# A graph network's opening phase: the encoder also skips block 11, and the early sums are dealt out anew

## What is computed

```python
h = jnp.maximum(_layernorm(x), 0.0)
h = jnp.maximum(h @ enc_w1.T + enc_b1, 0.0) @ enc_w2.T + enc_b2       # the encoder
def step(h, w):                                                       # five of these
    m = h @ w
    agg = jax.ops.segment_sum(m[src], dst, num_segments=n_nodes)      # a sum over edges
    gi = agg @ gru_wih.T + gru_bih
    gh = h @ gru_whh.T + gru_bhh
    ...
h, _ = jax.lax.scan(step, h, conv_w)
...
x = x + jax.nn.sigmoid(out)
...                                    # then the second network, with two more edge sums
```

## Time and profile before

| | us |
|---|---|
| median of three runs (745.25 to 745.31) | 745.26 |
| the profiled execution's own time | 745.62 |
| its span, first to last instruction | 743.3 |
| PE busy | 721.4 |
| DVE busy | 335.2 |
| ACT busy | 315.2 |
| clock granted to TensorE, mean | 0.999 of full |

### The profile page before, as it was taken

How to read it: one execution, slowest core, us unless ns; L and a number is a source line. 1 busy time by engine, 2 the same in 40 slices (tenths; PEclk the granted TensorE clock), 3 DMA queues, 4 the chain that set the end, 5 groups by cost and what they waited for, 6 DMA issues and landing times.

```text
span 743.3 us, 9918 instructions
## 1 busy us (share of the span) xinstructions
PE 721.4 (97%) x4071; PEld 394.4 (53%) x4071; DVE 335.2 (45%) x677; ACT 315.2 (42%) x463; POOL 44.5 (6%) x56
## 2 busy tenths in 40 slices
PE   6889999999999999999999999999999999999997
PEld 3556666445444444444444444444445545558886
DVE  7999999525023241123231223646644631123432
ACT  3977877645344344234452334432447421212000
POOL 4240000000000000000000000120002210000000
PEclk9999999999999999999999999999999999999999
DMA  5020000734102332022230212710002000000100
GB/s 164 6 84 16 4 2 5 147 69 81 9 1 55 63 51 46 1 48 39 53 75 0 49 37 38 115 63 2 1 0 97 9 1 1 1 1 6 34 31 25
DMA packets 79240, 28.41 MB, mean 38 GB/s; under 512 B 70519, under 2 KB 78390, under 8 KB 79062
## 3 DMA queue, kind: packets, MB, share of 16 engines
q1 hardware_dynamic: 78230, 26.93, 17.2%
q0 software_dynamic: 240, 0.66, 0.3%
q10 hardware_dynamic: 720, 0.13, 0.1%
HBM read 8.03 MB, written 2.60 MB: 14 GB/s over the span
## 4 chain that ended last, share of the span: by engine, by line
PE 85%; DVE 9%; ACT 2%; DMA 2%; POOL 1%; issue 1%; SPq 0%; DVEq 0%; ACTq 0%; POOLq 0%
PE PSA L1241 35%; PE PSA L1458 9%; PE PSA L1323 7%; PE PSA L1402 5%; PE PSA L1186 4%; PE PSA L1254 3%; PE PSA L1263 3%; PE PSA L1258 3%; PE PSA L1262 3%; PE PSA L1256 3%; PE PSA L1265 3%; DVE CT L869 3%; PE PSA L1390 2%; PE PSA L1378 1%; DMA H<-yS 1%; DVE stat L834 1%
## 5 line engine op out<-in xcount | busy, mean ns | idle before, releaser
L1241 PE MATMUL PSA<-AT,H 128*128 128x512 fp8e3 (+1 forms) x1470 | 275.8, 347 | 0.8 <-DMA H<-yS 0.8
L1241 PEld LDWEIGHTS PSA<-AT,H 128*128 128x128 f16 x1470 | 126.8, 98 | 151.9 <-issue 12.0
L1078 DVE SCALAR_TENSOR_TENSOR rS<-PSA,bias,rS 128x512 f32<-128x512 f32 (+1 forms) x35 | 23.9, 682 | 261.6 <-ACT rS L1635 261.6
L1635 ACT ACTIVATE rS<-PSA,bias 128x512 f32<-128x512 f32 (+1 forms) x35 | 22.1, 632 | 199.6 <-PE PSA L1262 199.6
L869 DVE TENSOR_TENSOR CT<-CT 128x2048 bf16<-128x2048 bf16 x80 | 91.4, 1206 | 0.0
L1565 ACT ACTIVATE AT<-PSA 128x1000 fp8e3<-128x1000 f32 (+1 forms) x79 | 74.4, 997 | 20.7 <-PE PSA L1186 20.5
L1539 ACT ACTIVATE CTL<-AT 128x3125 fp8e3<-128x3125 fp8e3 (+1 forms) x25 | 69.9, 2797 | 0.0
L1402 PE MATMUL PSA<-CT,H 128*128 128x512 fp8e3 (+1 forms) x336 | 65.5, 351 | 0.3 <-POOL H L762 0.3
L1458 PE MATMUL PSA<-AT,CT 128*128 128x256 f16 x576 | 65.1, 273 | 0.6 <-DVE AT L1040 0.6
L1458 PEld LDWEIGHTS PSA<-AT,CT 128*128 128x128 fp8e3 x576 | 55.4, 98 | 7.2 <-DVE AT L1040 0.8
L1323 PE MATMUL PSA<-AT,H 128*128 128x512 fp8e3 x245 | 58.0, 379 | 1.2 <-ACT AT L1565 1.2
(11 more groups left out here) (181 smaller groups left out, 661.8 us busy)
## 6 DMA issues: line engine op xcount, KB each, us to landing
AT<-scale_scratch SPq DMA_DIRECT2D x1, 1562.5 KB, 6.5
H<-in_x SPq DMA_DIRECT2D x1, 1536.0 KB
out<-AT SPq DMA_DIRECT2D x12, 128.0 KB
comb_scratch<-CT SPq DMA_DIRECT2D x1, 960.0 KB, 4.5
comb<-comb_scratch SPq DMA_DIRECT2D x5, 192.0 KB, 2.5
H<-yS SPq DMA_TRANSPOSE x48, 2.5
H<-in_x SPq DMA_DIRECT2D x1, 512.0 KB, 4.9
CT<-AT SPq DMA_TRANSPOSE x25, 4.0
```

What stands on the lines that cost most here:

```text
L1241: last = nc.tensor.matmul(bank[:, 0:w], H16[:, l % 2, t, h, :], AT3[:, t, n0:n0 + w], start=(t == 0 and h == 0), stop=(t == T - 1))
```

## The change

`REST` becomes a pair, so the encoder has no step in block 11 either, and every step from 11 on moves one block later. All that is tied to `block_of` moves along: `first_norm(6)` from block 10 to 11, `normalized(6)` from 11 to 12, and `low_encoded` of chunks 3 to 6 by one block each. `PART` deals the early sums out anew up to block 22: chunk 0's sum ends in block 20 instead of 18, and chunk 1's begins in block 16 instead of 13; from block 23 on nothing changes. ACT's copy of the first sum (`aggregated(0)`, L1627) follows from block 19 to block 21. The wait of `transposed_keys(2)` is set to the number of states that are written by then.

```diff
-        REST = 7
-        step = lambda b: b - ENC - (b > REST) if b != REST else None
+        REST = (7, 11)
+        step = lambda b: b - ENC - sum(b > r for r in REST) if b not in REST else None
...
-        PART = {7: [(0, 0, 4)], 8: [(0, 4, 8)], 10: [(0, 8, 12)], 12: [(0, 12, 16)], 13: [(1, 0, 4)], 14: [(0, 16, 20)],
-                15: [(1, 4, 8)], 16: [(0, 20, 24)], 17: [(1, 8, 11)], 18: [(0, 24, T), (1, 11, 13)]}
-        PART.update({19 + i: [(1, 13 + 3 * i, 16 + 3 * i)] for i in range(4)})
+        PART = {7: [(0, 0, 4)], 8: [(0, 4, 8)], 10: [(0, 8, 10)], 11: [(0, 10, 12)], 13: [(0, 12, 14)], 14: [(0, 14, 16)],
+                15: [(0, 16, 20)], 16: [(1, 0, 4)], 17: [(1, 4, 8)], 18: [(0, 20, 24)], 19: [(1, 8, 12)],
+                20: [(0, 24, T), (1, 12, 15)], 21: [(1, 15, 20)], 22: [(1, 20, T)]}
...
-                    pe.wait_ge(state_encoded, (3, 6, NC, NC)[k - 1])
+                    pe.wait_ge(state_encoded, (3, 5, NC, NC)[k - 1])
```

## The result

The changed kernel takes **750.53 us** (median of six runs, 747.92 to 751.13) against 745.23 for the kernel before in the same runs: a ratio of 1.0067, 95% interval 1.0056 to 1.0077, or **+5.3 us**. Forecast were +2.9 us and 747.0 to 749.3. The sign was right, the size was not, and the time lies above the range. The profiled execution took 750.48, its span is 748.3.

What follows compares the result with a forecast made beforehand. PE was taken as the bound from 64.5 us on, DVE just before. Lost early matmuls 2.59 plus a missing encoder step 0.62, less 0.27 already gained, gave +2.9 on 745.26: 748.2 us, range 747.0 to 749.3.

Steps and rivals of the forecast that it cites:

- The method: Opening blocks: sum PE's idle time from block 10 until it never waits again, 4.5 us against 1.45 before.
- DVE's dates: Blocks 12 and 13: DVE never idles, finishing block 12's one-hots at 56.55 and block 13's at 61.16 us.
- the key wait at L1215: Block 13: PE idles 1.6 us until ACT has copied the keys transposed just before.
- nothing behind block 22 absorbed or added anything: After block 14 PE runs without a gap, so the 2.9 us shift carries through to the end.
- So I add nothing: Stalls of 1.8 and 1.6 us on PE leave its clock at 2.4 GHz, so no time is added.
- the row from 5.7 to 11 us: Profile window of the kernel before: PE busy 2.05 of 5.30 us, clock granted at 1.00, cited against a clock fall.
- the prediction's dates: PE's expected times: block 13's one-hots at 61.29, L1215 going on at 64.25, block 14's head at 66.07 us.
- rival D: Clock falls in blocks 12 to 14, adding 3 to 5 us: 751 to 753 us, chance 0.07.
- stalls of 0.45, 1.8 and 1.6 us: PE idles 0.45 at L1228 in block 12, 1.8 ahead of block 13, 1.6 at L1215 in block 13.
- B: Chunk 1's old 1.34 us stall in block 13 goes and nothing replaces it: 743.9 us, chance 0.04.
- C: Later PE slack of some 3 us makes the moved matmuls free, leaving 0.3 us: 745.6 us, chance 0.07.
- handoffs: Five passes of work between engines, each good to 0.1 to 0.2 us, taken as unknowns beside the key wait.

Runs made afterwards that it cites:

- e1: The changed kernel plus seven unused 512-column matmuls in block 12, where PE idled ahead of block 13: 747.66 us, ratio 1.0034.
- e2: The kernel before, its encoder resting in block 7 only, with the new table of early sums: 746.07 us, ratio 1.0013.
- e3: The changed kernel's encoder pauses in blocks 7 and 11, with early sums as near to the old table as the waits allow: 746.68 us, ratio 1.0022.
- e4: The changed kernel with the third group's keys made in block 13 instead of 12, and the matching wait count: 746.05 us, ratio 1.0012.
- The halves: Two runs, each with one part of the change: the new table alone (e2), 746.07 us, and the encoder's second pause alone (e3), 746.68 us.
- r_after: The changed kernel measured again, unaltered, beside other runs on one chip: 750.56 us, ratio 1.0073.
- e8: The changed kernel with three tiles of chunk 0's early sum moved from blocks 13 to 15 into block 12, no work added: 747.07 us.
- e6: e1 with POOL's eight small memsets moved ahead of its last root: 747.63 us.

## Why the prediction was wrong

**The method held.** Idle time of PE up to the point from which it is saturated was the right sum, and it gave what it was to give wherever the clock stayed up: in e1, which is the changed kernel with its clock, the first L1254 came 3.03 us later than in before, for a forecast of 2.9 (by the time 747.66, for 748.2); e2, e3 and e4 came within 0.4 us, all on the low side. DVE's dates were right to 0.1 us but for POOL's memsets, which the prediction passed over: it moved POOL's last root, and not the memsets behind it, which then fell on the keys. Of the waits, the key wait at L1215 was foreseen with 1.6 and measured with 1.46 (e1), and in the changed kernel nothing behind block 22 absorbed or added anything: the first L1254 is 5.02 us later in the changed kernel (134.61 against 129.59), and the span 5.0 longer. The halves show that both parts of the change cost, and why: the table takes eight matmuls out of block 12, where DVE sets the date, and the pause brings the key copy and its reader into one block.

**The step that failed is the one on the clock.** "So I add nothing" stood on the row from 5.7 to 11 us, in which PE is busy 2.05 of 5.30 us and the column reads 1.00. That row did not show what it was read for, because PE was not at full speed there. The costs of the matmuls say so. These are rows of before:

```profile
7.39 1.58 PE L1163 MATMUL PSA<-CT 125*128 125x86 f32 x6 [1.22 <-DVE CT L807]
...
15.04 1.86 PE L1186 MATMUL PSA<-CT 128*128 128x125 bf16 x16
16.70 1.70 PE L1220 MATMUL PSA<-aggS,CT 128*128 128x512 f32 x2
18.23 1.11 PE L1186 MATMUL PSA<-CT 128*128 128x125 bf16 x16
```

and these are the same instructions in e1:

```profile
7.39 0.90 PE L1163 MATMUL PSA<-CT 125*128 125x86 f32 x6 [1.25 <-DVE CT L807]
...
15.02 1.86 PE L1186 MATMUL PSA<-CT 128*128 128x125 bf16 x16
16.68 2.02 PE L1220 MATMUL PSA<-aggS,CT 128*128 128x512 f32 x2
```

The windows at 15.04 cost 1.66 us from start to start, exactly as those of the changed kernel at 61.62 with its clock at 0.50, and not 0.96; and the six L1163, inside the row that the prediction used, took 1.58 us where e1 has them at 0.90. The trace of before has clock records only from 17.9 us on, and where there is no record the column reads 1.00. In e1 they begin at 6.0: full to 9.4, half to 19.6, then full. The windows from 11 to 20 us, of r_after (first record at 17.0) and then of e1, therefore look different for the same low level:

```profile
11.00:20.00 9.00, 5.46 (x40) 4.09 (x40) 8.86 (x27) 6.41 (x14) 3.14 (x2) 1.00 0.83 221
```

```profile
11.00:20.00 9.00, 6.60 (x40) 4.69 (x40) 8.86 (x27) 6.43 (x14) 3.17 (x2) 0.52 0.85 223
```

In both PE ran at half speed for most of that stretch, and the time did not suffer, since DVE, busy 8.86 of 9 us, sets the pace there. So the prediction had no row in which the clock was shown to hold with PE that idle. The least busy five microseconds of before in which it did hold are these, with 3.22 us of work, against 2.66 in the changed kernel ahead of the fall. That gives no limit; it says only that nothing so idle was on record:

```profile
39.00:44.00 5.00, 3.22 (x31) 2.03 (x32) 4.96 (x13) 2.84 (x5) 0.00 (x0) 1.00 0.54 197
```

What the runs showed in place of "nothing" is a clock of 0.50 from 61.4 to 68.2 us, for 2.0 us at block 14's head and at the first L1254.

By the rule of the Trainium skill that the prediction weighed ("TensorE: Matmul & The Clock Gate", HAM oscillation — how this bites in real kernels) the clock falls to half when PE is left waiting; the trace of the changed kernel agrees, with 0.50 from 61.5 to 68.2 us, although the waits of the page's example are longer than any here (1.52 us). The same page of the Trainium skill also says (What's actually happening) that the moment at which the clock rises moves from run to run; the traces agree, with the first full-speed record at 17.9 us in before, 17.0 in the changed kernel and 6.0 in e1, which run the same instructions up to there. That the fall too comes in one run and not in another is e8's finding.

**What the clock cost.** Behind 61.3 us, from the rows above, the changed kernel against the prediction's dates: block 13's head came 0.33 late, and that is the memsets, not the clock (e1 has it too, 61.59, and with the memsets moved, in e6, the keys take 1.52 us instead of 1.91). Then the slower windows delayed ACT's evictions and with them the key copy, so that L1215 restarted at 65.00 instead of 64.25, 0.42 more; L1215 cost 1.83 instead of 0.96, 0.87 more; the four early matmuls 1.55 instead of 0.86, 0.69 more. 0.33 + 0.42 + 0.87 + 0.69 = 2.31, which is all of 68.38 - 66.07. The clock's part is 1.98, and block 14's head in e1, at 66.39, says the same (1.99). The windows and the key transposes in the slow stretch took about 1.0 longer as well (from 61.62 to 63.84, 2.22 us, instead of 1.17), but PE would have waited for the key copy behind them anyway, so only 0.42 of it came through. That is why rival D's price of 3 to 5 was too high.

**The rivals.** D was the right one, and its chance of 0.07 rested on the misread row. The prediction itself had found stalls of 0.45, 1.8 and 1.6 us within eight, where the trace of before has no wait over 1.4 in the whole time from 17.9 us on. Its range of 751 to 753 missed the median from above. B failed where it was said to: in block 12, which has no work. C failed for the reason given: 40.00 of 40 us busy left nothing to absorb. The range was cut at 749.3 because only handoffs were let vary; a range that took the clock in would have reached 751.

## What to carry over

When a change takes work out of a stretch in which PE waits for another engine, sum up PE's idle time before and after, and then ask a second question: does PE still have enough to do there to keep its clock? Before a row of the profile is called as evidence, compare the cost of its matmuls with that of the same kind elsewhere, since the clock's column reads 1.00 where it has no record. Nor does one profile of the new kernel settle it (e8). A cheap way to find out is to fill the gap with matmuls into a free bank and see whether the time falls. And two instructions, one that hands data to another engine and one that waits for the answer, belong in different blocks (e4: the keys moved by one block, 4.4 us).

## What was not expected of the hardware

- Added work made the kernel faster: seven matmuls of 512 columns, 1.5 us of PE time, took 2.8 us off (5.3 us over before without them, 2.5 with them), 2.0 of it by the clock; two blocks later the same seven added 1.3.
- POOL's memsets of 0.1 to 0.3 us each stretched two DVE instructions from 0.22 and 0.28 to 0.72 and 0.65 us (L854, L855), while the L869 of before that met the same memsets kept its 1.2. The Trainium skill ("SBUF — State Buffer", Who interferes with whom) has it that a `tensor_scalar` in a two-port mode and GpSimd lock each other out of a shared pair of ports, and that a `tensor_tensor` meets only GpSimd's reads. L854 and L855 are the `tensor_scalar` among the six key instructions, L869 is a `tensor_tensor`; the trace agrees, and so does e6, in which the same memsets met L886, a `tensor_scalar` too. In before, on the other hand, L886 (54.31) began beside the last memset and kept its 0.33. That L854 and L855 ran in such a mode, and that it is these ports, was not tried.
- The clock's fall is not a property of the program alone: the same program (e8) had it in its profiled run and, by the times, in none of the other eight. Nor does an early recorded fall rule out the late one: by their means, the changed kernel's runs at 0.987 to 0.990 had both. What decides it in a given run stays open.
- A clock of 1.00 in the profile can be the lack of a record: from the start to 17.9 us the matmuls of before ran at half speed under a column that reads 1.00.
